# A post-norm decoder layer: the order of DVE's work in its first program, and the moves of the first norm to ACT and of the query's channel scale and bias behind the transposes

## The reference

```python
q, k, v = x @ Wq.T + bq, x @ Wk.T + bk, x @ Wv.T + bv        # self attention
phi_q, phi_k = elu(q) + 1, elu(k) + 1
context = phi_q * cumsum(phi_k * v, axis=1) * SCALE           # SCALE = 16 ** -0.5
x1 = layernorm(x + context @ Wo.T + bo)                       # over the 256 channels
sx = max(max|x1| / 127, 1e-8)   # one for each token;   qx = clip(round(x1 / sx), -127, 127)
sw = max(max|wq| / 127, 1e-8)   # one for each channel; qw = clip(round(wq / sw), -127, 127)
query = (qx @ qw.T) * (sx * sw) + xbq                         # then heads, scores, softmax, values
```

## Time and profile before

| | |
|---|---|
| Time, median of 3 runs (lowest to highest) | 834.48 us (833.97 to 837.61) |
| The profiled execution: its own time / its span | 835.97 us / 834.2 us |
| PE busy / weight loads busy | 741.3 us (89%) / 621.4 us (74%) |
| DVE / ACT / POOL busy | 513.1 (62%) / 505.9 (61%) / 224.4 us (27%) |
| Mean granted clock of PE | 0.942 |
| First program, from the span's start to SP's last issue | 73.3 us |

### The profile page before, as it was taken

How to read it: one execution, slowest core, us unless ns; L and a number is a source line. 1 busy time by engine, 2 the same in 40 slices (tenths; PEclk the granted TensorE clock), 3 DMA queues, 4 the chain that set the end, 5 groups by cost and what they waited for, 6 DMA issues and landing times. The chain is left out here.

```text
span 834.2 us, 18337 instructions
## 1 busy us (share of the span) xinstructions
PE 741.3 (89%) x7341; PEld 621.4 (74%) x7341; DVE 513.1 (62%) x993; ACT 505.9 (61%) x846; POOL 224.4 (27%) x176
## 2 busy tenths in 40 slices
PE   5745599999999999999999999999999999647954
PEld 2434388888888888888888888888888888436743
DVE  2886755565665566657656655666566556735655
ACT  4304157776677676767775776677677767523323
POOL 1020340413133131404040504051313310433633
PEclk9775899999999999999999999999999999959978
DMA  9008977887777778877887788778877755830421
GB/s 231 34 4 249 217 186 178 191 194 194 161 186 161 186 166 203 178 187 165 203 177 189 166 204 177 192 169 199 195 162 186 165 112 121 200 97 2 131 70 44
DMA packets 59891, 134.19 MB, mean 161 GB/s; under 512 B 24936, under 2 KB 43080, under 8 KB 59720
## 3 DMA queue, kind: packets, MB, share of 16 engines
q1 hardware_dynamic: 55632, 124.31, 63.9%
q0 software_dynamic: 2048, 7.34, 3.3%
q10 hardware_dynamic: 2128, 1.38, 0.6%
HBM read 53.50 MB, written 5.57 MB: 71 GB/s over the span
## 5 line engine op out<-in xcount | busy, mean ns | idle before, releaser
L1300 ACT ACTIVATE probsT<-ps_T 125x448 f32<-125x448 f32 x376 | 190.8, 541 | 160.1 <-PE ps_T L1179 144.9
L1396 DVE CUSTOM_DVE_ANT_0 scores<-ps_scores,mask_sb 112x1500 f32<-112x1500 f32 x128 | 219.7, 1717 | 94.6 <-PE ps_scores L1157 86.7
L1179 PE MATMUL ps_T<-ident,scores 112*128 112x112 f32 (+1 forms) x1536 | 196.5, 264 | 18.6 <-ACT probsT L1300 16.1
L1179 PEld LDWEIGHTS ps_T<-ident,scores 112*128 112x128 f32 (+1 forms) x1536 | 169.9, 146 | 54.1 <-ACT probsT L1300 36.9
L1288 ACT ACTIVATE scores<-scores,shift 112x1500 f32<-112x1500 f32 x128 | 197.0, 1541 | 3.7 <-DVE shift L1396 3.1
L1145 PE MATMUL ps_proj<-wkvT,room 128*125 128x256 f32 x1152 | 160.1, 288 | 0.0
L1138 PE MATMUL ps_proj<-room,wkvT 128*128 128x500 f32 x576 | 150.0, 406 | 8.4 <-DVE room L1483 8.4
L1073 POOL CAST room<-ctx_rows 128x1000 fp32r<-128x1000 f32 x45 | 45.8, 1019 | 401.1 <-PE ps_proj L1138 400.5
L1145 PEld LDWEIGHTS ps_proj<-wkvT,room 128*125 128x125 f32 x1152 | 141.8, 186 | 8.9 <-issue 8.1
L1138 PEld LDWEIGHTS ps_proj<-room,wkvT 128*128 128x128 f32 x576 | 106.7, 194 | 27.2 <-issue 8.7
L1157 PE MATMUL ps_scores<-k_stack,q_stack 96*112 96x500 f32 x384 | 118.1, 415 | 2.4 <-issue 1.7
(11 more groups left out here) (246 smaller groups left out, 489.5 us busy)
## 6 DMA issues: line engine op xcount, KB each, us to landing
k_stack<-room SPq DMA_DIRECT2D x384, 187.5 KB, 3.9
ctx_rows<-in_ctx SPq DMA_DIRECT2D x48, 500.0 KB, 5.6
mask_sb<-in_mask_BxSxS_ff SPq DMA_DIRECT2D x32, 328.1 KB
q_stack<-q_hi SPq DMA_DIRECT2D x32, 112.0 KB, 5.3
q_hi<-k_stack SPq DMA_DIRECT2D x4, 448.0 KB, 3.8
q_lo<-k_stack SPq DMA_DIRECT2D x4, 448.0 KB, 4.0
q_stack<-q_lo SPq DMA_DIRECT2D x16, 112.0 KB, 5.3
xT<-in_xT SPq DMA_DIRECT2D x2, 448.0 KB, 7.9
```

The lines of the kernel that those rows point to most:

```text
L1179: last = nc.tensor.transpose(ps_T[0:wide, (TB * t + k) % 2, j * PN:(j + 1) * PN], scores[:, t % 2, key:key + wide], keep["ident"][0:PN, 0:PN])
L1300: nc.scalar.activation(probsT[:, t % 2, k * TC:(k + 1) * TC], ps_T[0:LT, (TB * t + k) % 2, 0:TC * PN].rearrange("p (j n) -> p j n", j=TC), ...
L1396: nc.vector.tensor_tensor_reduce(out=split(scores[:, t % 2], NC), in0=ps_scores[0:PN, :, 0:LC], in1=split(mask_sb[:, a], NC), scale=-1.0, ...
```

## The change

- DVE starts its list with the chain of unit 0. The weight's scale (`query_weight_scale`) stands behind that chain, its integers (`query_weight_int`) behind that of u = 1; `weight_lo`, the gate and the atoms stand in gaps near the end.
- `bo` is no longer added to x on DVE: PE adds it to the output projection by a matmul of one row of ones with `bo_row`, one for each group.
- x1 is made by ACT for all 8 groups, `x * rstd + shift`; POOL makes `shift` = -mean * rstd, for each half right behind its rstd.
- ACT multiplies the queries by the token scale alone. Channel scale and bias come behind the turn: the turn is a plain matmul with the identity, added onto one with `diag` (bias over channel scale) and ones; `qbd_hi` and `qbd_lo` then multiply by `column_scale` (head mask x weight scale x SCALE). PE turns each half right behind its L327, ahead of the next half's `x_int`.
- The bias of the queries arrives by channel, and `bo_row` as one row. SP stores the gate between the two halves' queries.

```diff
@@ POOL @@
                     nc.gpsimd.tensor_tensor(rstd[:, g], var_eps[:, g], minus_half[:, g], ALU.pow).then_inc(rstd_ready, 1)
-                pool.wait_ge(rstd_ready, 2)
-                for i in range(HT + 1, NT):
-                    nc.gpsimd.tensor_scalar(keep["x1"][:, i], resid[:, i], mv[:, i, 0:1], rstd[:, i:i + 1],
-                                            ALU.subtract, ALU.mult).then_inc(x1_pool, 1)
+                    pool.wait_ge(rstd_ready, h + 1)
+                    pool.wait_ge(neg_mean_ready, h + 1)
+                    nc.gpsimd.tensor_tensor(shift[:, g], neg_mean[:, g], rstd[:, g], ALU.mult).then_inc(shift_ready, 1)
@@ PE, output projection @@
                     for i in range(h * HT, (h + 1) * HT):
+                        dst = ps[0:TT, i // 2, (i % 2) * D:(i % 2 + 1) * D]
+                        nc.tensor.matmul(dst, ones[0:1, 0:TT], bo_row[:], start=True, stop=False)
                         for m in range(KT):
...
@@ PE, queries, in the loop over h behind L327 @@
-                pe.wait_ge(row_ready, 1)
-                pe.wait_ge(x_intT_ready, 2)
-                for h in range(2):
-                    pe.wait_ge(query_ready, (h + 1) * HT)
+                    pe.wait_ge(diag_ready, KT)
+                    pe.wait_ge(q_scaled_ready, (h + 1) * HT)
                     for m in range(KT):
                         for j in range(HT):
-                            last = nc.tensor.transpose(ps[:, 4 + 2 * m + h, j * TT:(j + 1) * TT],
-                                                       query[:, h * HT + j, m * P:(m + 1) * P], keep["ident"][0:TT, 0:TT])
+                            dst = ps[:, 4 + 2 * m + h, j * TT:(j + 1) * TT]
+                            nc.tensor.matmul(dst, diag[:, m], ones[:, 0:TT], start=True, stop=False)
+                            last = nc.tensor.matmul(dst, q_scaled[:, h * HT + j, m * P:(m + 1) * P], keep["ident"][0:TT, 0:TT],
+                                                    start=False, stop=True)
                         last.then_inc(qT_in_psum, 1)
@@ ACT @@
+                for h in range(2):
+                    act.wait_ge(shift_ready, h + 1)
+                    for i in range(h * HT, (h + 1) * HT):
+                        nc.scalar.activation(keep["x1"][:, i], resid[:, i], ACT.Identity, scale=rstd[:, i:i + 1],
+                                             bias=shift[:, i:i + 1]).then_inc(x1_ready, 1)
+                act.wait_ge(column_ready, KT)
+                for h in range(2):
+                    for i in range(h * HT, (h + 1) * HT):
+                        if i % 2 == 0:
+                            act.wait_ge(q_in_psum, i // 2 + 1)
+                        nc.scalar.activation(q_scaled[:, i], ps[0:TT, i // 2, (i % 2) * D:(i % 2 + 1) * D], ACT.Copy,
+                                             scale=x_scale[:, i:i + 1]).then_inc(q_scaled_ready, 1)
+                    for m in range(KT):
+                        act.wait_ge(qT_in_psum, KT * h + m + 1)
...
@@ DVE @@
+                def query_weight_int():
...
+                    nc.vector.tensor_tensor(xbq_over[:], xbq[:], wq_inv[:], ALU.mult).then_inc(over_ready, 1)
+                    for m in range(KT):
+                        nc.vector.tensor_scalar(column_scale[:, m], head_mask[:], wq_scale[:, m:m + 1], SCALE, ALU.mult, ALU.mult).then_inc(column_ready, 1)
...
+                    for m in range(KT):
+                        nc.vector.tensor_scalar(diag[:, m], keep["ident"][:], xbq_over[:, m:m + 1], None, ALU.mult).then_inc(diag_ready, 1)
...
+                    if u == 0:
+                        query_weight_scale()
                     if u == 1:
+                        query_weight_int()
...
-                    if u == 2:
-                        weight_lo(XK)
-                weight_lo(XV)
...
+                    nc.vector.tensor_scalar(neg_mean[:, g], mv[:, g, 0], -1.0, None, ALU.mult).then_inc(neg_mean_ready, 1)
...
                     if h == 1:
-                        dve.wait_ge(row_ready, 1)
-                        scaled_query(0)
-                        scaled_query(1)
+                        weight_lo(XK)
                     dve.wait_ge(x_intT_in_psum, h + 1)
...
```

More of the change, by code:

```diff
@@ L109, in self_attention_phase @@
         ones = sb("ones", [P, TT])
[L110 removed]
+        column_scale = sb("column_scale", [P, KT, 2])
+        neg_mean = sb("neg_mean", [TT, NT])
+        shift = sb("x1_shift", [TT, NT])
         x_scale = sb("x_scale", [TT, NT])
@@ L118, in self_attention_phase @@
         head_mask = sb("head_mask", [P, 2])
-        query = resid
-        q_scaled = split(w_raw[0:TT].rearrange("p n k d -> p (n k d)")[:, 0:NT * D], NT)
+        q_scaled = split(free[:, NT * D // 2:NT * D // 2 + NT * D], NT)
         stacks = keep["k_stack"][:].rearrange("p k l -> p (k l)")
@@ L233, in _ @@
                         sp.dma_start(io["q_lo"][m, :, bs], qbd_lo[:, m, bs].bitcast(F32).rearrange("p b e n -> p b (e n)")).then_inc(q_stored, 16)
+                    if h == 0:
+                        sp.wait_ge(gate_steps, 2)
+                        sp.dma_start(wide(io["gate"]), keep["importance"][:]).then_inc(keep["gate_stored"], 16)
             @block.gpsimd
@@ L291, in _ @@
                 last.then_inc(wqT_in_psum, 1)
[L293 to L297, removed]
                 for h in range(2):
-                    pe.wait_ge(context_ready, KT * (h + 1))
                     if h == 0:
@@ L304, in _ @@
                         pe.wait_ge(v_used, 4)
+                        pe.wait_ge(row_in, 16)
+                        pe.wait_ge(dve_const, 2)
+                    pe.wait_ge(context_ready, KT * (h + 1))
                     for i in range(h * HT, (h + 1) * HT):
+                        dst = ps[0:TT, i // 2, (i % 2) * D:(i % 2 + 1) * D]
+                        nc.tensor.matmul(dst, ones[0:1, 0:TT], bo_row[:], start=True, stop=False)
                         for m in range(KT):
-                            last = nc.tensor.matmul(ps[0:TT, i // 2, (i % 2) * D:(i % 2 + 1) * D],
-                                                    context[:, m, i * TT:(i + 1) * TT], wT[:, WO, m], start=m == 0, stop=m == KT - 1)
+                            last = nc.tensor.matmul(dst, context[:, m, i * TT:(i + 1) * TT], wT[:, WO, m], start=False, stop=m == KT - 1)
                         if i % 2:
@@ L381, in _ @@
                 nc.scalar.activation(wq_intT[:], split(psb[:, 6, 0:KT * D], KT), ACT.Copy).then_inc(wqT_ready, 1)
[L382 to L390, removed]
+                for h in range(2):
[12 more added lines that the diff above has]
+                        act.wait_ge(qT_in_psum, KT * h + m + 1)
+                        for e in range(2):
+                            nc.scalar.activation(qbd_hi[:, m, batches(h), e], qT(m, h), ACT.Identity,
+                                                 scale=column_scale[:, m, e:e + 1]).then_inc(qbd_hi_ready, 1)
             @block.vector
@@ L407, in _ @@
[L407 to L412, removed]
```

113 lines of the change are left out of this document (47 added, 66 removed).

## The result

| | before | after |
|---|---|---|
| Time, median (lowest to highest) | 834.57 us (833.22 to 837.61, 9 runs) | 840.97 us (838.45 to 846.11, 9 runs) |
| The profiled execution: time / span | 835.97 / 834.2 us | 838.45 / 836.4 us |

What follows compares the result with a forecast made beforehand. PE is full from the fifth slice, so only shortening the first program, one long DVE chain, counts. Its end moves from 73.3 to 68.3: 5.0 us off 835.97 gives 831.0, median 829.5; range 826.8 to 834.3.

Steps and rivals of the forecast that it cites:

- Projections: First program's start: DVE's chains begin behind the exp, so the last kv ends at 30.1, 7.2 us earlier.
- Output projection: bo as a matmul makes 48 records instead of 32 on PE: 11.9 us, ending at 42.1 against 46.3.
- one cold stretch: In the output projection: the clock is low for some 3.4 us, as before, with 1.7 us to either side.
- the wholly cold 20 us: Output projection's 48 records if the clock stayed low throughout: 20 us, against the 11.9 taken.
- x1 off DVE: After the output projection: ACT makes x1, saving DVE 1.8 us; half 1's x1 is hidden by 0.8 us.
- Quantization: DVE's quantization of half 0, 50.59 to 56.0 before, takes about 0.6 us less without POOL beside it.
- Queries: PE's query turns: 32 records a half instead of 8; DVE waits some 5 us; lead 1 us at its lowest.
- SP: First program's end: SP is through its last store by 68.3 at 0.4 us an issue, 69.5 at 1.09.
- Sum: First program's end moves from 73.3 to 68.3, a gain of 5.0 us, so the median becomes 829.5 us.
- the slower one: Query turns: each record bound by its weight load, 0.31 us; turns 19.8 us against 9; 840.3 us; chance 0.06.

Runs made afterwards that it cites:

- e4: Kernel before plus one part: bo by a one-row matmul for each output-projection group, no addition of bo on DVE; time ratio 1.0104 to the kernel before.
- e1: Changed kernel with the output projection's bias matmul over 128 full rows (1/128 in each) instead of one; time ratio 0.9942 to the kernel before.
- e8: Kernel before with DVE's new order alone: first chain first, weight's scale behind it, integers behind the second, bo behind the last; ratio 0.9946 to the kernel before.
- e7: On e2, the whole query path put back as in the kernel before; new order and x1 on ACT stay; time ratio 0.9888 to the kernel before.
- e2: Changed kernel without the output projection's bias matmul, bo added to x by one DVE instruction behind the last chain; ratio 0.9942 to the kernel before.
- e5: On e2, query bias as 448-column matmuls issued earlier, half 1's x_int transposes between half 0's channel blocks; ratio 0.9872 to the kernel before.
- e9: Changed kernel with the output projection's bias matmul over 32 rows (1/32 in each) instead of one; time ratio 1.0077 to the kernel before.
- e10: Changed kernel with the output projection's bias matmul over 64 rows instead of one; time ratio 1.0062 to the kernel before.

## Why the prediction was wrong, by its steps

- **Projections**: right. 30.4 for the last kv where 30.1 was forecast. The first chain started at 14.90, not 14.2. The fifth bias column held ACT until 9.97, but the first Q relu waited for PE (12.62 instead of 12.02): PE started half a microsecond earlier than before, and its records stayed 0.75 us apart until 12.4 instead of 10.6. The prediction credits the new order with the gain; e4 has the start freed without it.
- **Output projection**: wrong, and this is the step that failed. "The clock came back by 42.0 after a start at 37.49 ... so I take one cold stretch" was read from stages in which every record used all 128 rows, and taken over to one in which a third of them use one. 22.8 us against 11.9. It had the wholly cold 20 us in hand and left it out of the range. With 40 of the 48 records cold the stage would be 18.8 us (40 x 0.427 + 8 x 0.216), so the clock makes 6.9 of the 10.9. The rest is a second term, which was missing: four records of a group take 0.13 us more when cold and 0.09 more when warm, 3.8 us in all. e1 gives the sum back as forecast, 12.1.
- **x1 off DVE**: right. (The prediction's 44.9 for the end of the statistics doesn't follow from its terms: 42.1 + 2.5 + 0.1 is 44.7.) Behind the stage 2.6 us to the maximum, and half 1's x1 was ready at 59.5 for 60.7.
- **Quantization**: right, 4.7 us between the maxima where 4.9 was taken.
- **Queries**: right in kind, 1.6 us short. The turn of half 0 ran cold for almost all of its 6.9 us, the clock rising at 70.5, where 5.7 were taken; DVE waited 6.2 where 5 were; half 1 ran at full clock, 3.8 us against 3.2. Records of the turn started 0.213 us apart cold and 0.112 warm, where 0.19 and 0.10 were taken: 0.7 and 0.4 us for 32. That the plain matmuls are what lifts the clock rested on the earlier trace rows, where PE was idle half of the time; e8's rise behind transposes speaks against a plain rule of that kind.
- **SP**: right; each issue took 0.32 us.
- **Sum**: 81.0 - 68.3 = 12.7 us, of which 0.4 ahead of the output projection, 10.9 in it, -0.2 from there to the maximum and 1.6 from the maximum to the end. The shift carried through the second program up to its last two score tiles.

Of the rivals, the slower one put a dear record in the queries; the mechanism was a cold clock in another stage, where the same prediction added matmuls of a kind that no row of before shows. L296 was full rows, and no one-row matmul was in the trace, so its effect on the clock had no nearest row. The wholly cold 20 us as a bound would have moved the range's end to about 838 (829.5 + 8.1). The rest up to 840.97 is in the main the price of the switches, which no row of before gives.

## What to carry to other kernels

A small operation moved to PE is paid in two coins: its records, and the clock of all records around it. A price taken from stages of full-row matmuls doesn't hold for a mixture, so take the wholly cold stage as an end of the range, and if a bias must go through PE, give it all rows (a constant of 1/128), if possible in one wide matmul placed where PE waits. And measure a bundle by its parts: here one part of four, by itself, lost 1.0% (e4) and hid the others. Of these the order alone wins 0.5% (e8), order and x1 on ACT with the old query path 1.1% (e7); with the new query path as it was written it is 0.6% (e2, and the two intervals just touch), and with PE's list put right 1.3% (e5), not clear of e7.

## What the runs showed of the hardware that was not expected

- Dense matmuls on 1, 32 or 64 of 128 rows for a third of the columns, between full ones, left the granted clock at 0.50 for 20 to 24 us (after, e4, e9, e10); with 128 rows it rose after 3.4 (e1).
- Where records of 1, 32 or 64 rows and records of 128 rows meet, successive fp32 records of 256 columns start 0.56 us apart instead of 0.43 at the cold clock and 0.31 instead of 0.215 at the warm one, twice at each change: across it and once behind it. The load of the first record behind a change, 0.26 us cold, starts with its record and not one record ahead (36.84 and 37.83 above). The Trainium skill ("TensorE: Matmul & The Clock Gate", Part 3) has loads overlap running matmuls only where the row group differs; here they overlapped between full-row records and not at the change. It isn't any change of the row count: the turn of the changed kernel goes between 128 and 112 rows at every second record, and all of them start 0.213 us apart when cold (64.15 to 70.34) and 0.112 when warm.
- The clock can rise behind transposes: in e8 after 1.93 us of bf16 matmuls and 1.73 us of fp32 transposes, dense, and 8 transposes then took 0.99 us instead of 1.73.
- The query weight and x landed 7.3 and 9.9 us after their issue with `bo` and the query bias as transfers of 1 KB (after), and 11.1 and 14.8 us after it with 112 KB each (before; e8 11.1 and 14.7). No run changes these transfers alone.
- Issues of the queries' stores cost SP 0.32 to 0.43 us each where they come in two batches (after), and 1.1 us for the last four where eight come close together (e4, e8).
